# Attention and mixture-of-experts layer on one core: front with biases and residual added by matmul, output projection in plain float32

## What is computed

```python
QKV = X @ W_in.T + b_in;  Q, K, V = split(QKV)        # 3 x 256 features
Q = rope(Q, 128); K = rope(K, 128)                     # first 128 features turned
A = sum over tokens of (K / max(|K|, 1e-12)) * V       # one vector of 256
Y = (A * Q) @ W_out.T + b_out + X
x = layernorm(X + Y)                                   # so X enters twice
w = top-2 routing weights of softmax(x @ gate_w), times alpha   # 8 experts
F = sum_e w[:, e] * (gelu(x @ fc1_w[e] + fc1_b[e]) @ fc2_w[e] + fc2_b[e])
out = layernorm(x + F)
```

## Time and profile before

| | |
|---|---|
| time, median of 3 runs | 152.05 us (151.35 to 152.91) |
| span of the profiled execution | 150.5 us |
| its device time beside that | not given apart; the runs lie 0.85 to 2.4 us above the span |
| busy: PE, weight loads, DVE, ACT, POOL | 135.8, 118.9, 105.7, 77.3, 67.6 us |
| moved by DMA | 10.55 MB |

### The profile page before, as it was taken

How to read it: one execution, slowest core, us unless ns; L and a number is a source line. 1 busy time by engine, 2 the same in 40 slices (tenths; PEclk the granted TensorE clock), 3 DMA queues, 4 the chain that set the end, 5 groups by cost and what they waited for, 6 DMA issues and landing times.

```text
span 150.5 us, 2427 instructions
## 1 busy us (share of the span) xinstructions
PE 135.8 (90%) x802; PEld 118.9 (79%) x802; DVE 105.7 (70%) x233; ACT 77.3 (51%) x146; POOL 67.6 (45%) x81
## 2 busy tenths in 40 slices
PE   4999979955999899999999999999999999999920
PEld 4778859825987579897898998998998998989910
DVE  0549899996598938899955965745965654638991
ACT  4515966017076894168064264264265265297571
POOL 3004899913999807048306606707507606000310
PEclk9999997555599999999999999999999999999996
DMA  4899940000003130004000400400300000000034
GB/s 133 213 321 419 387 185 4 0 0 0 2 4 121 44 119 0 0 0 139 4 0 0 139 4 2 139 0 0 139 0 0 0 0 0 4 0 0 0 121 158
DMA packets 4698, 10.55 MB, mean 70 GB/s; under 512 B 545, under 2 KB 2641, under 8 KB 4433
## 3 DMA queue, kind: packets, MB, share of 16 engines
q1 hardware_dynamic: 4688, 10.43, 20.1%
HBM read 9.38 MB, written 1.05 MB: 69 GB/s over the span
## 4 chain that ended last, share of the span: by engine, by line
PE 64%; DVE 20%; DMA 5%; ACT 3%; SPq 3%; issue 1%; ACTq 0%; DVEq 0%
PE ps L878 21%; PE ps L879 20%; PE ps L880 20%; DMA wq<-in_w_q_t 5%; DVE z L607 4%; DVE qa L648 2%; DVE kv L588 2%; SPq L257 2%; DVE x L727 2%; DVE z L678 1%; ACT gT_lo L425 1%; DVE stats L849 1%; DVE fT_lo L699 1%; DVE qb L656 1%; DVE acc L752 1%
## 5 line engine op out<-in xcount | busy, mean ns | idle before, releaser
L738 DVE TENSOR_TENSOR gT_lo<-kv,gT_hi 128x512 fp32r<-128x512 f32 x30 | 26.1, 884 | 26.1 <-ACT gT_hi L509 26.0
L352 POOL TENSOR_TENSOR w_hi<-wraw,zero 128x512 fp32r<-128x512 f32 x16 | 18.9, 1181 | 41.2 <-PE ps L880 41.2
L878 PE MATMUL ps<-w_hi,gT_hi 128*128 128x256 f32 x120 | 33.7, 281 | 0.1
L880 PE MATMUL ps<-w_hi,gT_lo 128*128 128x256 f32 x120 | 33.4, 279 | 0.0
L879 PE MATMUL ps<-w_lo,gT_hi 128*128 128x256 f32 x120 | 33.4, 278 | 0.0
L878 PE MATMUL ps<-fT_hi,w_hi 128*128 128x512 f32 x64 | 25.5, 399 | 0.3 <-DVE fT_lo L699 0.3
L879 PE MATMUL ps<-fT_lo,w_hi 128*128 128x512 f32 x64 | 25.4, 396 | 0.0
L880 PE MATMUL ps<-fT_hi,w_lo 128*128 128x512 f32 x64 | 25.3, 395 | 0.0
L507 ACT ACTIVATE kv<-ps,b_now 128x512 f32<-128x512 f32 x16 | 11.0, 690 | 24.7 <-PE ps L880 24.5
L878 PEld LDWEIGHTS ps<-w_hi,gT_hi 128*128 128x128 f32 x120 | 22.7, 189 | 1.1 <-issue 0.4
L752 DVE SCALAR_TENSOR_TENSOR acc<-ps,comb,acc 128x256 f32<-128x256 f32 x53 | 22.6, 475 | 1.0 <-PE ps L880 0.7
(11 more groups left out here) (139 smaller groups left out, 243.1 us busy)
## 6 DMA issues: line engine op xcount, KB each, us to landing
wraw<-in_expert_w SPq DMA_DIRECT2D x8, 512.0 KB, 3.4
xT<-in_x_t SPq DMA_DIRECT2D x4, 256.0 KB, 5.6
acc<-in_x_tok SPq DMA_DIRECT2D x1, 1024.0 KB, 9.5
rT<-in_rope_t SPq DMA_DIRECT2D x1, 1024.0 KB, 10.8
out<-z SPq DMA_DIRECT2D x4, 256.0 KB, 2.2
wkv<-in_w_kv_t SPq DMA_DIRECT2D x2, 256.0 KB, 3.6
rtok<-in_rope_tok SPq DMA_DIRECT2D x1, 512.0 KB, 7.8
brow<-in_b_rows SPq DMA_DIRECT2D x1, 384.0 KB, 6.4
```

The source lines that it names most:

```text
L352: g.tensor_tensor(w_hi[:, slot, cols], src, zero[:].to_broadcast([P, 2 * D]), ALU.add).then_inc(w_part, 1)
L738: v.tensor_tensor(low, h[:, i, :], raw(high), ALU.subtract).then_inc(g_lo_ok, 1)
L878: nc.tensor.matmul(dst, lh, rh, start=k == 0, stop=False)
L880: last = nc.tensor.matmul(dst, ll, rh, start=False, stop=k == len(terms) - 1)
```

## The change

- K and V: a seventh matmul per tile adds the bias: a stationary matrix `pick` (ones in rows 0 and 32) by `b_parts` (row 0 the bias's high part, row 32 its low part). `b_rows` is now an array of 33 rows, loaded to `braw`; POOL makes `b_parts`. PE's tile 0 waits for `b_lo_ok`, POOL's last step.
- K's norm, V's copy and K times V are taken from PSUM: ACT squares K there and copies V to `vs`, DVE multiplies three times (whole, and the two rotary halves crossed, `m2`). The rotation is done behind the product: by cosine and by sine, two instructions for each group, into `acc`, on POOL and for tile 7 on DVE; the sums of the parts are left to PE, with three one-column matmuls per tile instead of two.
- PE's order: kv tiles 0 to 3, both Q blocks of the first half, kv tiles 4 to 7, one Q block, all eight feature sums, the last Q block.
- Q: DVE adds the bias and multiplies by the tables straight from PSUM; no high and low parts of Q are made.
- Output projection: two plain float32 matmuls of 256 columns per tile (`qT` by `wo_a`) instead of six of float32r; into the same PSUM go first 2X + b_out (`residual`: four float32r matmuls with twice the identity, `twice`, and one with `pick`). `x_tok` is no longer loaded, `first_sum` is gone; statistics and normalisation read PSUM. The first norm's transposes are cut two tiles at a time. The five `stay_warm` matmuls ahead of the first expert are gone.
- Loads: pieces 0 and 1 of `x_t` are issued by ACT; the rotary table comes as `cs` and `sn`; POOL makes minus the sine, and the zeroing of `gpad` and `comb_p` moves behind it. ACT loads its table for the root at the start.

The core of the diff:

```diff
-            sp.dma_start(brow[:], b_rows.partition_broadcast(P)).then_inc(l_brow, 16)
+            for k in range(KD):
+                sp.dma_start(wkv[:, k, :], w_kv_t[:, k, :]).then_inc(l_wkv[k], 16)
             load_x_t(2)
+            sp.dma_start(braw[:], b_rows).then_inc(l_bias, 16)
             load_x_t(3)
-            sp.dma_start(acc[:], x_tok).then_inc(l_x, 16)
...
+            pool.wait_ge(l_bias, 16)
+            pool.wait_ge(b_zero, 1)
+            g.tensor_copy(b_parts[0:BIAS_K, :], braw[:]).then_inc(b_hi_ok, 1)
+            pool.wait_ge(b_hi_ok, 1)
+            g.tensor_tensor(b_parts[low, :], braw[low, :], raw(b_parts[low, :]), ALU.subtract).then_inc(b_lo_ok, 1)
...
+            def v_out(t):
+
+                a.copy(vs[:, t, :], ps[:, KV_BANK[t], D:2 * D]).then_inc(v_ok, 1)
...
+            def kv_product(t):
+
+                bank = KV_BANK[t]
                 dve.wait_ge(ksq_ok, t + 1)
...
+                dve.wait_ge(v_ok, t + 1)
+                v.tensor_tensor(z[:, t, :], ps[:, bank, 0:D], vs[:, t, :], ALU.mult).then_inc(m_ok, 1)
+                v.tensor_tensor(m2[:, t, EVEN], ps[:, bank, ODD], vs[:, t, EVEN], ALU.mult).then_inc(turn_ok, 1)
+                v.tensor_tensor(m2[:, t, ODD], ps[:, bank, EVEN], vs[:, t, ODD], ALU.mult).then_inc(turn_ok, 1)
...
+                if t == 0:
+                    pe.wait_ge(pick_ok, 2)
+                    pe.wait_ge(b_lo_ok, 1)
+                nc.tensor.matmul(ps[:, bank, :], pick[:], b_parts[:, 0:2 * D], start=False, stop=True).then_inc(kv_mm, 1)
...
+                nc.tensor.matmul(rest, z[:, t, ROT:D], norm, start=t == 0, stop=t == T - 1)
+                nc.tensor.matmul(rot, acc[:, t, 0:ROT], norm, start=t == 0, stop=False)
+                return nc.tensor.matmul(rot, acc[:, t, ROT:D], norm, start=False, stop=t == T - 1)
...
+            def residual(t):
+
+                z_t = z_ps(t)
+                for k in range(KD):
+                    nc.tensor.matmul(z_t, fT_hi[:, k, tile(t)], twice[:, k, :], start=k == 0, stop=False)
+                    nc.tensor.matmul(z_t, fT_lo[:, k, tile(t)], twice[:, k, :], start=False, stop=False)
+                nc.tensor.matmul(z_t, pick[:], b_parts[:, 2 * D:3 * D], start=False, stop=False)
...
+                for k in range(KD):
+                    last = nc.tensor.matmul(z_ps(t), qT[:, k, tile(t)], wo_a[:, k, :], start=False, stop=k == KD - 1)
+                last.then_inc(o_mm, 1)
...
-            x1_transpose(2)
-            x1_transpose(3)
-            stay_warm(WARM_NORM)
```

More of the change, by code:

```diff
@@ new lines, in _ @@
+            pool.wait_ge(diag_ok, KD)
+            g.tensor_copy(twice[:], twice_raw[:]).then_inc(twice_ok, 1)
+            low = slice(BIAS_K - 1, BIAS_K)
+            pool.wait_ge(l_bias, 16)
[3 more added lines that the diff above has]
+            g.tensor_tensor(b_parts[low, :], braw[low, :], raw(b_parts[low, :]), ALU.subtract).then_inc(b_lo_ok, 1)
+            pool.wait_ge(b_lo_ok, 1)
@@ L410, in x_high @@
                 a.copy(fT_hi[:, :, part], xT[:, :, part]).then_inc(xT_hi_ok, 1)
+            for c in range(2):
+                part = slice(c * 256, (c + 1) * 256)
+                act.dma_start(xT[:, :, part], x_t[:, :, part]).then_inc(l_xT[c], 16)
+            act.wait_ge(const_ok, 1)
+            a.activation(table_unused[:, 0:1], eps[:], ACT.Sqrt)
             for k in range(KD):
@@ L658, in q_rotate @@
[L658 to L671 removed]
+            k_reciprocal(1)
@@ L913, in feature_sum @@
-            def feature_sum(n):
-                pe.wait_ge(krec_ok, n + 1)
-                for t in range(n * TPH, (n + 1) * TPH):
-                    pe.wait_ge(kv_prod, t + 1)
-                    for k in range(KD):
-                        last = nc.tensor.matmul(ps[:, 2 + k, 0:1], z[:, t, tile(k)], krec[:, t:t + 1],
-                                                start=t == 0, stop=t == T - 1)
-                return last
+                    nc.tensor.matmul(ps[:, bank, :], f_hi, wkv_hi[:, k, :], start=k == 0, stop=False)
@@ new lines, in kv_tile @@
+                    nc.tensor.matmul(ps[:, bank, :], f_hi, wkv_lo[:, k, :], start=False, stop=False)
+                    nc.tensor.matmul(ps[:, bank, :], f_lo, wkv_hi[:, k, :], start=False, stop=False)
+                if t == 0:
+                    pe.wait_ge(pick_ok, 2)
+                    pe.wait_ge(b_lo_ok, 1)
+                nc.tensor.matmul(ps[:, bank, :], pick[:], b_parts[:, 0:2 * D], start=False, stop=True).then_inc(kv_mm, 1)
+            def q_block(n, m):
+                product(ps[:, Q_BANK[n][m], :], [(wq_hi[:, k, tile(m)], wq_lo[:, k, tile(m)],
+                                                  fT_hi[:, k, half(n)], fT_lo[:, k, half(n)]) for k in range(KD)])\
+                    .then_inc(q_mm, 1)
@@ L923, in _ @@
+            for t in range(TPH):
+                kv_tile(t)
             pe.wait_ge(wq_lo_ok, 1)
```

468 lines of the change are left out of this document (226 added, 242 removed).

## The result

The changed kernel takes **159.9 us** by the median of its four executions, one of which took 355 us for a reason that the record does not show; the other three took 158.37, 159.54 and 160.26. The kernel before beside it takes 151.7 (151.27 to 152.91): a ratio of **1.049**, 95% interval 1.042 to 1.057. It is slower, by 8.2 us (7.8 by the median of the three), where 7.5 were forecast. The profiled execution took 160.26, its span is 158.3.

What follows compares the result with a forecast made beforehand. PE was taken to bound the experts, so any shift of the second gate block reaches the end: 60.2 - 52.68 = +7.5 us, span 158.0, plus 1.55 from span to median, 159.5 us; range 156 to 162.

Steps and rivals of the forecast that it cites:

- Step 1: Tile 0: PE waits 3.2 us (0 to 4.3) for the bias parts, ready at 11.9.
- Step 2: Kv tiles 1 to 7 and three Q blocks: done at 28.4, with 0.6 us lost to the clock after the pause.
- Step 3: Feature sums, 48 records in one piece: 7.3 us, to 35.7, the last 16 records at the lower clock.
- Step 4: Fourth Q block and projection: 14.5 us at full clock plus 2.9 lost at half, ending at 53.1.
- the rival of cheap float32: Projection: each float32 record is bound by its weight load, 3.8 us instead of 7.3, total 156; chance 0.09.
- the sentence that the late one is PE itself: Projection stage: the 3.51 us wait goes, and PE's own 14.5 us of work is what is late next.
- the rival that I had given 0.14: Behind the projection: PE waits for the first norm and the clock falls a third time, about +3.5 us, 163; chance 0.14.
- Step 5: Statistics, normalisation, transposes and parts of the last two tiles: 7.1 us (4.6 to 8.4), second gate block at 60.2.
- one of my own signs of being wrong: Signs against the forecast: bias wait under 1 us, projection records near 0.12 apart, gate block before 55, PE idle inside experts.
- The account by difference: Cross-check on PE: 10.0 us more work, 4.7 of waits and 1.3 of warming lost, a 3.2 wait gained: +7.2.
- The rival of the holding clock: Front: the clock stays up, decided at the 48 one-column sum records; gate block at 53.6, total 153.0; chance 0.12.

Runs made afterwards that it cites:

- e1: The changed kernel with the bias matmuls of kv tiles 0 to 3 issued behind tile 3's own matmuls; 156.85 us, ratio 1.031 to the kernel before.
- e3: The changed kernel with 14 identity matmuls, whose result nobody reads, put ahead of the first bias matmul; 158.79 us, ratio 1.038 to the kernel before.
- e5: The changed kernel with qT and wo_a as float32r, so that a projection matmul is one record instead of two; 160.0 us, ratio 1.042 to the kernel before.
- e4: The changed kernel without the 40 residual records, so 2X + b_out is left out of its result; 158.13 us, ratio 1.022 to the kernel before.
- the three of b: The kernel before with only the projection in plain float32, run twice (149.86 and 150.2 us), and once with Q's parts still made but unread (151.7 us).
- e2: The changed kernel with the feature sums of tiles 0 to 3 issued one at a time behind kv tiles 4 to 7; 159.26 us.
- e7: The changed kernel with three places of the first norm reordered on PE, ACT and DVE, same instructions; 158.05 us, ratio 1.033 to the kernel before.
- e9: The changed kernel with the orders of e1 and e7, plus wq_lo earlier, sums split and Q blocks moved, same instructions; 151.27 us, ratio 0.989 to the kernel before.
- b1: The kernel before with only the output projection changed to plain float32, without parts of Q and scaled W_out; 149.86 us, ratio 0.985 to the kernel before.
- b1_again: The same kernel as b1, run a second time; 150.2 us, the kernel before beside it 151.44.

## Why the prediction was right, and where its reasons were not

That the span came within 0.3 us of the forecast (158.3 against 158.0) is in part luck: the sums began 1.75 us late, the sums and the projection then took 2.1 us less than forecast, and the experts added 0.9 that the sum did not have. The stated range, 156 to 162, is also narrower than the bounds of its steps added up (about 150 to 167).

**Step 1, the pause.** Forecast 3.2 us, the bias matmul at 11.9; measured 3.61 and 11.99. The tile ended 0.3 and the load landed 0.6 earlier than taken, POOL's pair took 3.5 us instead of 2.7. e1 and e3 show that the pause is what it was said to be.

**Step 2, kv tiles and Q blocks.** The term most mis-sized. The fall of the clock in the pause was put at 0.6 us out of 0 to 2.4; the first bias matmul and the tiles 1 to 3 took 7.7 us instead of 5.0 at full clock, 2.7 lost, and the first Q block began at 19.71 where 17.3 was forecast. `wq_lo` was ready at 17.9, so only 1.8 of the 2.7 counts; the sums started at 30.15, forecast 28.4.

**Step 3, the sums.** Forecast 7.3, measured 6.0 (30.15 to 36.15). The clock fell in them, but only for the last few records. This made up for most of step 2: 36.15 against 35.7.

**Step 4, the projection.** Forecast 17.4 us with 2.9 at half clock; measured 16.6 (36.15 to 52.75), the clock back 5.4 us after the fourth Q block began, 2.7 lost, no wait for `wo_a`. A float32 record lasted about as long as a 512-column one (group of PE by form, changed kernel, 40 to 54 us):

```profile
L937 PE MATMUL ps<-wo_a,qT 128*128 128x256 f32 x32 | 8.3, 387 | 0.0
```

A projection tile with its residual took 1.46 us from 44.22, of which 5 x 0.12 are the residual, so a matmul 0.43, forecast 0.46. That rules out the rival of cheap float32 (0.24). The four passes that the prediction cites from the Trainium skill's "FP8 and Floating Point Precision" gave 0.43: the trace agrees.

But the sentence that the late one is PE itself was only half right. It holds for the kernel as it is (PE waits 1.43 us in the stage) and fails in the profiled executions in which PE has less to do: e5 took 16 records away for nothing, e4 40 records for 0.84 us at the gate block (about 4 us by its ratio, so for e4 the size is open). Both times the norm's chain took over and the clock fell a third time, the rival that I had given 0.14; in the changed kernel itself, with 1.43 us of standing, it did not.

**Step 5, the norm.** Forecast 7.1, measured 6.9, the gate block at 59.62 instead of 60.2. The experts then did not run quite as before: PE stands 0.96 us ahead of the second product (`fc2_pair`) of expert 1, counted from 0, at 77.42, which I did not foresee, and PE idle inside the experts was one of my own signs of being wrong. The kernel before does not show it, nor do e1, e4, e5 and the three of b; e2, e3, e7 and e9 do. The span grew by 0.86 more than the gate block moved (158.3 - 59.62 = 98.68 against 150.5 - 52.68 = 97.82), and in e1, e4 and e5, without it, that rest is 98.1 to 98.3. PE, then POOL and DVE ahead of it, in the changed kernel:

```profile
77.42 0.36 PE L856 MATMUL ps<-w_hi,gT_hi 128*128 128x256 f32 x1 [0.96 <-issue]
```

```profile
75.73 1.04 POOL L347 TENSOR_TENSOR w_hi<-wraw,zero 128x512 fp32r<-128x512 f32 x1 [0.43 <-PE ps L858]
75.77 1.55 DVE L712 TENSOR_TENSOR gT_lo<-vs,gT_hi 128x512 fp32r<-128x512 f32 x1
```

The same two in e1, where PE does not stand:

```profile
72.73 1.57 POOL L347 TENSOR_TENSOR w_hi<-wraw,zero 128x512 fp32r<-128x512 f32 x1 [0.48 <-PE ps L858]
72.73 0.68 DVE L712 TENSOR_TENSOR gT_lo<-vs,gT_hi 128x512 fp32r<-128x512 f32 x1
```

The profile names no releaser, but the kernel does: this matmul waits for the second low part of expert 1 (`g_lo_ok` at 6), which is the DVE instruction shown and ends at 77.32. All twelve traces divide the same way. In the five with the 0.96 us that instruction takes 1.55 or 1.56 us and the one of POOL beside it 1.04; in the seven without, it takes 0.68 or 0.69 and POOL's 1.57 to 2.29. One of the two holds the other up, and PE stands when the late one is DVE's. In the changed kernel and its variants the two begin within 0.04 us of each other, so a very small shift decides; no run set it on purpose.

**The account by difference** (10.0 us of work for PE, less waits, plus a new wait) gave +7.2 and so looked like a cause. It is none. e9 keeps all the work and is faster than the kernel before; and I counted the dearer projection as 1.5 us of loss, while b1 shows the new projection alone as a gain of 1.2 to 2.9 us by the medians, since it takes work off POOL and DVE ahead of the sums' copy. So the change is two changes. The projection without parts helps; the rebuilt front with the residual by matmul costs about 10 us against b1 (159.9 against 149.9 and 150.2; ratios 1.049 and 0.985): 3.0 in the pause (e1), 1.3 at the gate block in the order of the norm (e7), and with the other moves of e9 all but 1.4 us (151.27 against 149.86). How the rest divides between the earlier `wq_lo`, the split sums and the clock was not measured apart, since e9 moved them together.

The rival of the holding clock fell by its own point: the clock did not hold through the sums, and it fell even earlier, in the pause. e9 shows what it would have been worth, with the waits gone too.

## What to carry to other kernels

Before counting what a change gives the busiest engine, place it: ten microseconds of matmuls added behind work that is ready cost little here (e9), while a 3.6 us pause ahead of a small operand cost itself and a stretch at half clock. When an engine is taken to be the bound, ask what stands right behind it; a wait of 1.4 us in the same stage already says that part of the work taken off it can come back as waiting. And price a removed operation not by its own engine's time but by what it stood ahead of, and by whose port it held.

## What the runs showed of the hardware

- POOL's time went by columns and not by partitions: 2.12 us for a subtraction of 768 columns on one partition, 0.74 for 256 columns on 16.
- The granted clock fell in the pause ahead of the first bias matmul, whether that was 2.76 us long (e4), 3.44 to 3.74 (e7, the changed kernel, e2) or 4.54 (e5), and at the end of those of 3.45 and 3.56 ahead of the first expert block (e4, e5). It stayed up in pauses of 1.26 to 2.73 (e3, the changed kernel, e2, e1) and in one of 2.99 (b1), behind which it fell 1.0 us later. So the length of the pause alone does not tell what the clock will do. It also fell in a run of one-column matmuls with PE busy for 17 us before (34.7 in the changed kernel); e3, which kept it up at 11, had it fall at 30.3 instead. Its place differs between two executions of one kernel (b1 and b1_again).
- A stretch at half clock cost nothing where a wait stood behind it: b1_again ran its fourth Q block at half and began the projection no later than b1.
- Two instructions of 512 columns, on DVE and on POOL, that began within 0.04 us of each other took 1.55 and 1.04 us in some kernels and 0.68 and 1.57 in others. It cost PE 0.96 us or nothing.
